# Pass two of a fused feed-forward kernel: block products summed in PSUM, two of them one step later

## The reference, cut to what matters

```python
h = layernorm(x) * (1 + ca) + sa
x = x + ga * (h @ w_masked.T)
h = layernorm(x) * (1 + cb) + sb
w1, w2, w3 = dequant_nf4(...)            # HIDDEN 2752, 64 values to a scale
h = silu(h @ w1.T) * (h @ w2.T)
x = x + gb * (h @ w3.T)
```

## Time and profile before

| | |
|---|---|
| median of 3 runs | 1570.92 us (1569.18 to 1571.37) |
| span of the profiled execution | 1567.6 us |
| PE busy | 1539.4 us, 98% of the span |
| DVE busy | 1029.5 us, 66% |
| ACT busy | 989.6 us, 63% |
| DMA, mean | 221 GB/s |
| first and last matmul of pass two | 733.94 us, 1144.44 us |

### The profile page before, as it was taken

How to read it: one execution, slowest core, us unless ns; L and a number is a source line. 1 busy time by engine, 2 the same in 40 slices (tenths; PEclk the granted TensorE clock), 3 DMA queues, 4 the chain that set the end, 5 groups by cost and what they waited for, 6 DMA issues and landing times.

```text
span 1567.6 us, 19154 instructions
## 1 busy us (share of the span) xinstructions
PE 1539.4 (98%) x7200; PEld 1269.6 (81%) x7200; DVE 1029.5 (66%) x1486; ACT 989.6 (63%) x1290; POOL 5.5 (0%) x10
## 2 busy tenths in 40 slices
PE   5899999999999999999999999999999999999999
PEld 3688888888888888888888888888888888888887
DVE  5687786555555455547676666666875757956994
ACT  3475676998888888884898988785433432333220
POOL 0000000000000000000000000000000000000000
PEclk9999999999999999999999999999999999999999
DMA  9976423564555445532778787786777868947973
GB/s 368 372 258 228 134 81 138 177 200 166 186 169 187 153 162 180 178 128 97 257 228 252 207 250 208 207 254 171 260 292 272 332 204 302 343 160 268 397 279 122
DMA packets 170139, 345.97 MB, mean 221 GB/s; under 512 B 14752, under 2 KB 65344, under 8 KB 170048
## 3 DMA queue, kind: packets, MB, share of 16 engines
q1 hardware_dynamic: 170048, 344.76, 65.1%
HBM read 249.77 MB, written 94.93 MB: 220 GB/s over the span
## 4 chain that ended last, share of the span: by engine, by line
PE 96%; DMA 2%; DVE 0%; ACT 0%; SPq 0%; issue 0%
PE ps L1916 10%; PE ps L1915 10%; PE ps L1914 10%; PE ps L1988 9%; PE ps L1987 9%; PE ps L1989 9%; PE ps L1925 9%; PE ps L1927 9%; PE ps L1926 9%; PE ps L1832 4%; PE ps L1834 4%; PE ps L1833 4%; DMA wmod<-wmod 2%; PE ps L1789 2%; PE ps L1772 1%; DVE attn_w_lo L1368 0%
## 5 line engine op out<-in xcount | busy, mean ns | idle before, releaser
L861 ACT ACTIVATE w_raw<-w_raw 128x1024 f32<-128x1024 f32 x287 | 304.6, 1061 | 9.1
L1914 PE MATMUL ps<-ffn_in_hi,w_hi 128*128 128x512 f32 x688 | 268.6, 390 | 0.0
L1916 PE MATMUL ps<-ffn_in_hi,w_lo 128*128 128x512 f32 x688 | 267.8, 389 | 0.0
L1915 PE MATMUL ps<-ffn_in_lo,w_hi 128*128 128x512 f32 x688 | 267.7, 389 | 0.0
L1987 PE MATMUL ps<-t_hi,s_hi 128*128 128x512 f32 x616 | 239.6, 389 | 0.0
L1988 PE MATMUL ps<-t_lo,s_hi 128*128 128x512 f32 x616 | 239.6, 389 | 0.0
L1989 PE MATMUL ps<-t_hi,s_lo 128*128 128x512 f32 x616 | 239.6, 389 | 0.0
L1925 PE MATMUL ps<-x_m_hi,stream_hi 128*128 128x512 f32 x604 | 235.0, 389 | 0.0
L1926 PE MATMUL ps<-x_m_lo,stream_hi 128*128 128x512 f32 x604 | 235.0, 389 | 0.0
L1927 PE MATMUL ps<-x_m_hi,stream_lo 128*128 128x512 f32 x604 | 235.0, 389 | 0.0
L1114 ACT ACTIVATE s_hi<-s_raw 128x1408 fp32r<-128x1408 f32 x56 | 77.4, 1383 | 241.2 <-DVE s_raw L1624 192.6
(11 more groups left out here) (136 smaller groups left out, 2078.1 us busy)
## 6 DMA issues: line engine op xcount, KB each, us to landing
s_raw<-h_d SPq DMA_DIRECT2D x96, 704.0 KB, 5.6
stream_raw<-t_d SPq DMA_DIRECT2D x150, 256.0 KB, 3.4
t_d<-combined SPq DMA_DIRECT2D x106, 256.0 KB, 2.6
wmod<-wmod SPq DMA_DIRECT2D x12, 2048.0 KB, 15.3
t_raw<-w_d SPq DMA_DIRECT2D x88, 256.0 KB, 6.1
w_codes<-w12q SPq DMA_DIRECT2D x41, 512.0 KB, 5.3
h_d<-h_tile SPq DMA_DIRECT2D x44, 256.0 KB, 2.4
h_d<-up_c SPq DMA_DIRECT2D x44, 256.0 KB, 3.3
```

The costliest lines, as they stand in the source:

```text
L861: act.activation(RAWF[r], RAWF[r] if j else RQ[r][:], ACT.Prelu, bias=bias, scale=sign, alpha=slope).then_inc(line_ready, 1)
L1914: pe.matmul(acc, RH[r][:, k, :], HH[:, b, k, :], start=(k == 0), stop=False)
L1915: pe.matmul(acc, RH[r][:, k, :], HL[:, b, k, :], start=False, stop=False)
L1916: last = pe.matmul(acc, RL[r][:, k, :], HH[:, b, k, :], start=False, stop=(k == C - 1))
```

## The change

The products of a step are added onto one another in PSUM. A step has three banks instead of seven: one takes m5, then m3, then m6; one takes m2, then m4, then m7; one takes m1. Even steps have banks 2 to 4, odd steps banks 5 to 7. Between two products of one bank the intermediate sum is read. Every product after the first in a bank has `start=False`. m7 and m6 of step c are issued inside step c+1, behind its m5, m2 and m1:

```diff
+    OPEN, CLOSE, MIDDLE = ("m5", "m2", "m1"), ("m7", "m6"), ("m4", "m3")
+    def step_products(c):
+        return [(c, n) for n in OPEN] + [(c - 1, n) for n in CLOSE if c] + [(c, n) for n in MIDDLE]
+
+    END_PRODUCTS = [(FULL, 0), (FULL, 1), (FULL - 1, "m7"), (FULL - 1, "m6"), (FULL, 2), (FULL, 3)]
...
     def up_bank(c, name):
-        return (NU * c + 2 + UP_AT[name]) % 8
+        return 2 + 3 * (c % 2) + {"m5": 0, "m3": 0, "m6": 0, "m2": 1, "m4": 1, "m7": 1, "m1": 2}[name]
...
+                if name == "m5":
+                    if c >= 2:
+                        pe.wait_ge(up_c_step, c_at(c - 2, "c22"))
+                    else:
+                        pe.wait_ge(silu_done, made(END, c))
...
+                elif name == "m4":
+                    pe.wait_ge(up_copied, 2 * c + 1)
+                elif name == "m3":
+                    pe.wait_ge(up_c_step, c_at(c, "e"))
+                elif name == "m7":
+                    pe.wait_ge(up_copied, 2 * c + 2)
+                else:
+                    pe.wait_ge(silu_done, H0 + 2 * c + 1)
```

VectorE has four operations a step instead of eight: `both_used` ("e", m5 plus the copy of m2), `first_left` ("f", m1 subtracted), `finish_c11` (after m7) and `finish_c22` (after m6). ScalarE copies the bank after m2 and after m4, and takes the silu of one batch straight out of PSUM after m3. VectorE's loop, and ScalarE's order around the first step:

```diff
+            for c in range(1, FULL - 1):
+                for q in stream_step(c + 1)[:3]:
+                    stream_low(*q)
+                both_used(c)
+                for q in stream_step(c + 1)[3:5]:
+                    stream_low(*q)
+                first_left(c)
+                for q in stream_step(c + 1)[5:]:
+                    stream_low(*q)
                 for j in w3_ended(c - 1)[:1]:
                     w3_combine(j)
+                finish_c11(c - 1)
                 for j in w3_ended(c - 1)[1:]:
                     w3_combine(j)
+                finish_c22(c - 1)
+                make_h_up(c - 1, 1)
+                make_h_up(c - 1, 0)
...
+            for q in stream_step(1)[3:]:
+                stream_high(*q)
+            for q in w3_steps(0):
+                w3_step(q)
+            for c in range(1, FULL - 1):
+                copy_up(c - 1, "m4")
+                silu_up(c - 1, 1)
```

More of the change, by code:

```diff
@@ L699, in _ @@
                     sp.wait_ge(first_stored, 32)
-                    for i in range(2):
-                        load_stream(0, i)
+                    for name in OPEN[:2]:
+                        load_stream(0, name)
                     for r in range(4):
@@ L710, in _ @@
             load_s3(0)
-            for i in range(NU):
-                load_stream(1, i)
+            for name in OPEN + MIDDLE + CLOSE:
+                load_stream(1, name)
             load_w3_codes(0)
@@ L723, in _ @@
                 for i in range(NU):
[L724 to L728, removed]
+                    if c + 2 <= FULL and i < len(stream_step(c + 2)) and stream_step(c + 2)[i][0] >= 2:
+                        load_stream(*stream_step(c + 2)[i])
                     if c == 0 and i in (0, 3):
@@ L742, in _ @@
                             finish_w3(j)
[L743 to L757, removed]
+            sp.wait_ge(up_m_done, up_done(FULL - 2, "m1"))
+            load_t(0, 2)
+            sp.wait_ge(up_m_done, up_done(FULL - 1, "m2"))
+            load_t(0, 4)
+            sp.wait_ge(up_m_done, up_done(FULL - 1, "m1"))
+            for b in range(2):
+                for par in range(2):
+                    sp.wait_ge(h1_stored[b][par], 16 * (6 - par))
+            load_s(0)
+            load_t(0, 5)
+            sp.wait_ge(up_m_done, up_done(FULL - 2, "m6"))
+            load_t(0, 3)
+            for b in (1, 0):
+                store_h_up(FULL - 2, b)
+            sp.wait_ge(up_m_done, up_done(FULL - 1, "m7"))
+            for m in range(1, 4):
+                load_s(m)
             for b in (1, 0):
                 store_h_up(FULL - 1, b)
-            sp.wait_ge(up_m_done, NU * FULL + 2)
-            load_s(3)
             for b in range(2):
@@ L1054, in copy_up @@
             def copy_up(c, name):
-                p, i = c % 2, UP_AT[name]
-                act.wait_ge(up_m_done, NU * c + i + 1)
+                p, b = c % 2, 1 if name == "m2" else 0
+                act.wait_ge(up_m_done, up_done(c, name))
                 if c == 0:
[L1058 to L1063, removed]
+                    act.wait_ge(ts_stored[3 - b], 16 * len(range(3 - b, len(SUMS), 4)))
@@ L1080, in _ @@
+            for name in OPEN[:2]:
+                stream_high(0, name)
             silu(FULL, 0)
@@ L1517, in _ @@
             x_low("m4")
-            for i in range(2, NU):
-                stream_low(0, i)
+            for name in OPEN[2:] + MIDDLE:
+                stream_low(0, name)
             x_add("m7")
@@ L1559, in use_m3, with both_used @@
[L1559 to L1570, removed]
+            def both_used(c):
+                dve.wait_ge(up_copied, 2 * c + 1)
+                step_up(CU[c % 2], bank(c, "m5"), CU[c % 2][:], ALU.add)
@@ new lines, in first_left, with finish_c11 @@
+            def first_left(c):
+                dve.wait_ge(up_m_done, up_done(c, "m1"))
+                dve.wait_ge(up_c_step, c_at(c, "e"))
+                step_up(CU[c % 2], bank(c, "m1"), CU[c % 2][:], ALU.subtract)
+            def finish_c11(c):
+                p = c % 2
+                dve.wait_ge(up_m_done, up_done(c, "m7"))
+                dve.wait_ge(up_c_step, c_at(c, "f"))
+                if c >= 2:
+                    dve.wait_ge(h_made, H0 + 2 * (c - 1))
+                else:
+                    dve.wait_ge(xc_added, X_READ)
+                step_up(CT_[p], bank(c, "m7"), CU[p][:], ALU.add)
@@ L1572, in make_h_up, with finish_c22 @@
+            def finish_c22(c):
+                p = c % 2
+                dve.wait_ge(up_m_done, up_done(c, "m6"))
+                dve.wait_ge(up_c_step, c_at(c, "c11"))
+                step_up(CU[p], bank(c, "m6"), CU[p][:], ALU.add)
             def make_h_up(c, b):
@@ L1964, in _, with tail_product @@
+                block_product(ps[:, up_bank(c, name), :], TT[c % 2][UP_AT[name]], name, name in OPEN, True, name not in OPEN)
+            def tail_product(n):
+                a, x, b = TAIL_PARTS[n]
                 if n != 2:
-                    pe.wait_ge(tt_lo, stream_at(FULL, UP_AT[a]) + 1)
+                    pe.wait_ge(tt_lo, stream_at(FULL, a) + 1)
+                if n == 0:
+                    pe.wait_ge(up_c_step, c_at(FULL - 2, "c22"))
                 block_product(ps[:, tail_bank(b), :], TT[FULL % 2][UP_AT[a]], x, n % 2 == 0, n % 2 == 1)
+            for c, name in UP_PRODUCTS:
+                if c == FULL:
+                    tail_product(name)
+                else:
+                    up_product(c, name)
@@ L1971, in down_tile @@
                 if m == 0:
[L1972 removed]
+                    pe.wait_ge(h_made, H0)
+                elif m == 2:
+                    pe.wait_ge(up_c_step, c_at(FULL - 1, "c22"))
                 if m < 8:
```

251 lines of the change are left out of this document (114 added, 137 removed).

## The result

| | before | changed |
|---|---|---|
| median | 1570.37 us (1569.18 to 1571.37, 4 runs) | 1589.77 us (1587.64 to 1590.43, 4 runs) |
| ratio | 1 | 1.0123 (95%: 1.0111 to 1.0136) |
| span of the profiled execution | 1567.6 us | 1585.9 us |

The changed kernel is 1.2% slower; the forecast was 1588.0 in a range of 1580 to 1594. The profiled execution is the fastest of its four. In every run whose time and span are both on record, the time is 1.7 to 1.8 us above the span; the 3.3 us between the median before and its profiled span are therefore not all time around the span. The forecast doesn't hang on it, since it adds the lost time to the median. The spans differ by 18.3 us, and pass two, from its first matmul to the first of the down projection, went from 410.72 to 428.9 us: all of the difference lies there.

What follows compares the result with a forecast made beforehand. TensorE, 98% busy and without a gap in pass two, was taken as the bound, so only new waits count: 9.6 + 1.7 + 3.7 + 2.1 = 17.1 us on 1570.92 gives 1588.0 us, eight in ten within 1580 to 1594.

Steps and rivals of the forecast that it cites:

- The frame: Pass two: TensorE has no gap and the same 1812 matmuls, so nothing to win; only new waits count.
- The start: m7 of step 0 waits for ScalarE's copy behind nine w3 activations: 9.6 us, including m5 of step 1.
- Not on top of it: The 2.1 us stand at m5 of step 1 lies inside the start's 9.6 us, leaving 7.5 before m7.
- The clock: Behind the 7.5 us stand before m7, matmuls run at the 1.2 GHz level: 1.7 us once.
- twice, if it falls again: Upper bound of the clock's cost: 2 x 1.7 us if the clock falls twice.
- The step starts: m5 waits for finish_c22 behind the second w3 scaling: three times 1.0 us and one 0.7, sum 3.7.
- The end: First product of the down projection waits for s_low(0) on VectorE, with two products ahead: 2.1 us.
- Only the start: Rival, 0.12: waits of m5 and of the end are covered; 9.6 + 1.7 remain, 1582.2 us.
- no wait at the start: Rival, 0.05: ScalarE reaches step 0's copy in time; 2.1, 3.7 and 2.1 us remain, 1578.8 us.
- waits hidden altogether: Rival, 0.02: all the new waits are hidden.
- ScalarE as the bound in every step: Rival, 0.06: TensorE stands about 1 us in each of 18 steps, 35 us in all, 1606 us.
- Faster through fewer reads of PSUM: Rival, 0.01: 63 fewer PSUM reads give 3.8 us back and new waits are hidden, 1567.1 us.

Runs made afterwards that it cites:

- the loads earlier: No w3 in step 0, c22 first, end chain moved ahead, plus step 1's m5 and m2 loads ahead of the last store_h; 1570.16 us, 1.0000 to before.
- the second profile: Profiled execution of the changed kernel measured again, unaltered, with the follow-up runs; median 1588.38 us, ratio 1.0114 to the kernel before, span 1587.9 us.
- no w3 in step 0: c22 first, plus step 0's w3 activations spread over steps 1 to 17; 1578.25 us, ratio 1.0045 to the kernel before.
- c22 first: Changed kernel with finish_c22 ahead of the second w3 scaling in VectorE's order; 1584.30 us, ratio 1.0093 to the kernel before.
- copy first: Changed kernel with ScalarE's copy and silu of step 0 ahead of the nine w3 activations; 1583.66 us, ratio 1.0085 to the kernel before.
- five ahead: Changed kernel with five of step 0's nine w3 activations ahead of the copy after m4, four behind; 1584.93 us, ratio 1.0096 to the kernel before.
- end only: Changed kernel with s_add(0), s_high(0) and s_low(0) ahead of the last finish_c22; 1585.69 us, ratio 1.0100 to the kernel before.

## Why the prediction was right, point by point

**The frame held.** VectorE lost 51 us of busy time (about 50 said) with no effect, and the pitch of the matmuls stayed at 0.227 us. The experiment with the loads earlier shows it from the other side: without the new waits the time is that of before.

**The start: 9.6 said, 9.3 measured** (765.00 - 755.70), of which 2.22 at m5 of step 1 (2.1 said) and the rest before m7, where the wait row has 6.65 us and the prediction's sign was 7 to 8. "Not on top of it" is shown: when the first stand came with a slow clock, the second became shorter by as much. The copy ended at 764.85, 0.5 before the 765.3 said.

**The clock: 1.7 said, 2.0 measured**: ten matmuls at 0.427 instead of 0.227 us between 765.0 and 769.4. The prediction named some 3 us at 0.50; it was 4.4 us of work, and the fall began in the stand, not behind it. The bound "twice, if it falls again" was the right one to keep: it did so in the second profile.

**The step starts: 3.7 said, 3.4 waited** (0.89, 0.87, 0.46 and 1.22 in time order). The sum was good, the split less so: the three full tiles were taken as 1.0 each and took 0.9, 0.9 and 0.5, and the fourth, with half a tile, was taken as 0.7 and took 1.2, the longest. Its one load is waited for nearly as long as the two of a full tile (5.54 against 6.13 us), and behind the wait stands a memset of 0.91 us that the others have not. The chain itself came as predicted: at the place shown, the second scaling starts 6.7 us after the first has ended (6.8 said). The experiment that moves the addition took away all four.

**The end: 2.1 said, 2.03 measured**, 2.7 by the run that changes it alone.

**What the sum left out.** The wait rows and the clock give 9.3 + 2.0 + 3.4 + 2.0 = 16.7, and pass two is 18.2 longer. A wait row says less than the time lost. Its idle is counted from the end of the last matmul (0.39 us after its start), while the next would have started after 0.227: 0.16 us. And the first matmul behind a stand has its successor 0.31 us behind it instead of 0.227 (855.28, 855.59): 0.08. The start is free of the first part, being counted from 755.70. For the four step starts it is 4 x 0.24, for the end 0.16 and for m7's first matmul 0.13 (0.56 us to its successor, where the slow pitch is 0.427): 1.25 us in all, so 18.0 of the 18.2.

The prediction counted its stands from the time at which the next matmul was due, so the 0.16 is inside its terms. Counted its way, the step starts were 1.04, 1.02, 0.62 and 1.38 us late, 4.1 against 3.7 said (at the one shown, 855.28 - 854.01 - 0.227), and the end was 2.2 late against 2.1. With 9.3 for the start and 2.0 for the clock that makes 17.6 against the 17.1 said; the remaining 0.6 is the slow first matmul behind each stand, which the sum did not have. So the sum is close because each term is, and only a little because errors cancel: the start was put 0.3 too high, the other three terms 0.8 too low, and 0.6 was missing.

**The rivals.** Only the start (1582.2), no wait at the start (1578.8) and waits hidden altogether fall by the wait rows, in which all four places stand. ScalarE as the bound in every step (1606) falls, as its copy is waited for once in 21 steps; with no w3 in step 0 it has even more to do in each later step and is not waited for at all. Faster through fewer reads of PSUM (1567.1) falls by the pitch, and by the ratio 1.0000 of the kernel that has the fewer reads and no new wait.

## What to carry to other kernels

Where an engine already runs without a gap, a change that leaves its work the same can only add waits: follow each new wait back through the in-order queue of the engine it names and add up what stands ahead. Moving the awaited instruction ahead of the backlog mends that one wait and hands the backlog to the next one (4.5 us of the 18 came back in the profile, 2.1 of them from a clock that happened to hold); only taking the backlog out of the tight stretch removed it. And count a stand from the start of the last matmul plus its pitch, as the prediction did, not from its end; with the slow first matmul behind it, a stand here costs 0.24 us more than its wait row says.

## What the runs showed of the hardware

**Stands of 2.0 to 3.2 us sometimes bring the slow clock and sometimes not, at the same place in the same kernel.** Behind the first stand of step 1 the clock fell in the second profile of the changed kernel (2.24 us) and in that of "c22 first" (2.35), and stayed at 1.00 in the first profile (2.22), in "copy first" (2.31), in "five ahead" (2.33) and in "end only" (2.02). At the first product of the down projection one stand of 2.02 us had a fall, and five of 2.02 and 2.03 had none. "Copy first" has a stand of 3.20 us before m4 of step 1 without a fall:

```profile
768.00:770.00 2.00, 2.00 (x11) 1.64 (x10) 2.00 (x5) 2.00 (x4) 0.00 (x0) 1.00 0.00 0
```

Before, one of 3.20 us had one. All stands of 4.6 us and more in pass two had a fall in these profiles (6.65, 6.17, 4.80, 4.59), and none under 2.0 had (from 772 to 1156 us no window of 4 us is below 0.99 in any of the traces). The Trainium skill says in "TensorE: Matmul & The Clock Gate", section "HAM oscillation — how this bites in real kernels", that a wait between bursts can put the array back to half rate, so that the next burst starts cold; the runs agree for the long stands, and of the 14 between 2.0 and 3.2 us in pass two and at its end, three had a fall.

**A fall costs 1.3 to 2.0 us** where nothing later absorbs it (seven to ten matmuls at 0.427 us), and nothing where a stand follows that something else ends. The two profiled executions of the changed kernel fit it: 2.0 us apart, of which the fall at the end is 1.6 and the first product of the down projection is 0.33 later.

**Whether falls are what spreads the runs is not shown.** In "c22 first" the record fits it: the two runs of 1582.7 and 1583.1 us have a mean granted clock of 0.996, those of 1585.5 and 1585.8 one of 0.992. In "no w3 in step 0" it does not: the three runs of 1578.1 to 1578.6 us have 0.997 and 0.998, the profiled one of 1574.0 us has 0.998, while the profiles with one to three falls in or behind pass two have 0.994 to 0.996. What made those three runs 4 us longer stays open. Nor do the ranges settle it: with one stand left ten runs spread over 4.1 us and with none eleven over 2.4, but the kernel before, which has no stand in pass two, spread over 3.6 us on the chip of the former and 2.4 on that of the latter.
